# Attention: score stacks loaded in two column parts, first-pass tiles ordered by query tile, projections and statistics moved between steps

## What is computed

```python
qkv = x @ Wqkv.T + b_qkv                        # 16 heads of 32
scores = einsum('bqhd,bkhd->bhqk', q, k) * scale + alibi_bias
scores = where(causal, scores, -1e9)
p = softmax(scores, axis=-1)
ctx = einsum('bhqk,bkhd->bqhd', p, v)
return ctx @ Wout.T + b_out
```

## Time and profile before

| | us |
|---|---|
| median of 3 runs | 3004.56 (3004.28 to 3004.92) |
| the profiled execution | 3000.08 |
| its span | 2998.4 |

### The profile page before, as it was taken

How to read it: one execution, slowest core, us unless ns; L and a number is a source line. 1 busy time by engine, 2 the same in 40 slices (tenths; PEclk the granted TensorE clock), 3 DMA queues, 4 the chain that set the end, 5 groups by cost and what they waited for, 6 DMA issues and landing times. The chain is left out here.

```text
span 2998.4 us, 67154 instructions
## 1 busy us (share of the span) xinstructions
PE 2562.4 (85%) x13156; PEld 1885.8 (63%) x13157; DVE 1534.4 (51%) x3734; ACT 1375.9 (46%) x3572; POOL 1099.5 (37%) x913
## 2 busy tenths in 40 slices
PE   0229999999999378989989898998599999999994
PEld 0117888888888245555555555555378888888883
DVE  8764554555543336564564646455345555555431
ACT  0216666666655323232232323232166666666652
POOL 3434655565555200001011010101245655555552
PEclk9999999999999778998989888898799999999997
DMA  5436877888854423232332323333167787888545
GB/s 154 134 125 156 189 179 179 188 186 185 193 94 53 100 57 79 78 76 74 92 85 77 80 71 78 85 78 86 60 170 179 187 189 170 189 192 197 96 55 144
DMA packets 155637, 377.83 MB, mean 126 GB/s; under 512 B 33277, under 2 KB 34685, under 8 KB 155298
## 3 DMA queue, kind: packets, MB, share of 16 engines
q0 software_dynamic: 76416, 168.58, 29.0%
q1 hardware_dynamic: 68256, 198.28, 23.1%
q10 hardware_dynamic: 10882, 10.14, 1.1%
HBM read 236.63 MB, written 126.88 MB: 121 GB/s over the span
## 5 line engine op out<-in xcount | busy, mean ns | idle before, releaser
L504 POOL DMA_INDIRECT x_rows<-f_ob,f_it x320 | 514.3, 1607 | 573.3 <-ACT f_ob L651 240.0
L554 PE MATMUL f_psg<-f_wh,f_xh 128*128 x1280 | 535.4, 418 | 4.7 <-DVE f_xl L722 4.7
L554 PE MATMUL f_psg<-f_wh,f_xl 128*128 x1280 | 504.9, 394 | 0.0
L554 PE MATMUL f_psg<-f_wl,f_xh 128*128 x1280 | 502.1, 392 | 0.0
L496 POOL DMA_INDIRECT f_xg<-xn_rows,f_it x320 | 356.4, 1114 | 112.6 <-issue 94.5
L1309 DVE CUSTOM_DVE_ANT_0 a_psa<-a_psa,cst 128x128 f32<-128x128 f32 (+3 forms) x512 | 249.8, 504 | 189.2 <-PE a_psa L1096 186.6
L1225 ACT ACTIVATE a_pt<-a_psb 128x256 f32<-128x256 f32 (+3 forms) x512 | 213.3, 438 | 284.4 <-PE a_psb L1144 279.6
L1017 POOL CAST a_cth<-a_ct 128x512 fp32r<-128x512 f32 x32 | 19.6, 612 | 798.5 <-DVE a_ct L1333 798.5
L651 ACT ACTIVATE f_ob<-f_pso,f_wcol 128x512 f32<-128x512 f32 x320 | 220.7, 690 | 192.5 <-issue 116.1
L1096 PE MATMUL a_psa<-a_stk,a_stq 98*128 98x128 f32 (+3 forms) x512 | 230.5, 458 | 79.0 <-DVE a_mx L1309 41.9
L722 DVE TENSOR_TENSOR f_xl<-f_psx,f_xh 128x512 fp32r<-128x512 f32 x320 | 221.4, 692 | 137.3 <-ACT f_xh L632 90.7
(11 more groups left out here) (186 smaller groups left out, 4383.6 us busy)
## 6 DMA issues: line engine op xcount, KB each, us to landing
f_wraw<-w_in SPq DMA_DIRECT2D x128, 768.0 KB
a_stq<-a_qk SPq DMA_DIRECT2D x128, 192.0 KB
a_stk<-a_qk SPq DMA_DIRECT2D x128, 192.0 KB
r_xt<-x_in SPq DMA_DIRECT2D x32, 256.0 KB, 4.4
xn_rows<-r_xo SPq DMA_DIRECT2D x32, 256.0 KB, 2.9
a_xt<-x_rows SPq DMA_DIRECT2D x8, 1024.0 KB, 5.2
a_x<-x_rows SPq DMA_DIRECT2D x8, 1024.0 KB, 5.5
x_rows<-a_x POOLq DMA_DIRECT2D x8, 1024.0 KB, 5.0
```

What stands on the lines that cost most here:

```text
L504: g.indirect_dma_start(x_d, bass.IndirectOffsetOnAxis(it[:, n:n + 1], 0), ob[:, n % OB, :], None, compute_op=ALU.add).then_inc(s_sca[n % O ...
L554: mm = pe.matmul(psg[:, j, :], x[:, j, k, :], w[:, cols], start=(k == 0 and n == 0), stop=(k == DC - 1 and n == 2))
```

## The change

1. Stacks are loaded in two column parts: columns 0 to 383 of all rows once B tiles 0 to 11 of the slot's old owner are done, then columns 384 to 511 once all 16 are; ten DMAs each, so 20 per u instead of 10, of 3/4 and 1/4 the size. Each part has its own semaphore (`s_stk`, `s_stl`); `high` waits for both.
2. A tiles run by query tile (four heads of 128 columns, then of 256, 384, 512), two per step in steps 0 to 2 and one per step in 3 to 12. Tile 0 waits for part one, tile 12 (the first with 512 columns) for part two.
3. `turn_maxima` is in step 15, ahead of the last context products; the values of the next batch come after it.
4. q of u+2 is projected ahead of the steps as before, k in four chunks of three products in steps 0, 1, 3 and 5.
5. ScalarE makes high of q after exp 1 and high of k after exp 7; VectorE makes low of q after maximum 4, low of k after maximum 11. The statistics are placed one tile at a time after maxima 5, 7, 9 and 12 (the last with the moments). The turns of x are in steps 9, 10, 12 and 14; VectorE's rows after maxima 5, 6, 8, 9 and the low halves after 12 to 15. VectorE's `normalise` always comes after `negated`.

```diff
+    LATE = S - P
+    A_AT = {0: (0, 1), 1: (2, 3), 2: (4, 5), 3: (6,), 4: (7,), 5: (8,), 6: (9,), 7: (10,), 8: (11,), 9: (12,),
+            10: (13,), 11: (14,), 12: (15,)}
+    K_AT = {0: 0, 1: 1, 3: 2, 5: 3}
+    X_AT = {9: 0, 10: 1, 12: 2, 14: 3}
+    STATS_AT = {5: (0,), 7: (1,), 9: (2,), 12: (3, TB)}
+    ROW_AT, LOW_AT = {5: 0, 6: 1, 8: 2, 9: 3}, {12: 0, 13: 1, 14: 2, 15: 3}
...
                     sp.wait_ge(s_qh, u + 1)
-                    if not below(u, 2):
-                        sp.wait_ge(s_b, u * 16 - 16)
-                    for j in range(HG):
-                        rows = slice(j * HD, (j + 1) * HD)
-                        for n, to in enumerate((stq, stk)):
-                            sp.dma_start(raw(to[0:3 * HD, slot + j, :]), raw(qk3[rows, n, :, :])).then_inc(s_stk, 16)
-                    for r in range(2):
...
+                    for done, cols, told in ((12, slice(0, LATE), s_stk), (16, slice(LATE, S), s_stl)):
+                        if not below(u, 2):
+                            sp.wait_ge(s_b, u * 16 - (32 - done))
+                        for j in range(HG):
+                            rows = slice(j * HD, (j + 1) * HD)
+                            for n, to in enumerate((stq, stk)):
+                                sp.dma_start(raw(to[0:3 * HD, slot + j, cols]), raw(qk3[rows, n, :, cols])
+                                             ).then_inc(told, 16)
+                        for r in range(2):
...
+                def scores_row(u, slot, *tiles):
+
+                    for i in tiles:
+                        t, h = i // HG, slot * HG + i % HG
+                        if i == 0:
+                            pe.wait_ge(s_stk, u * STK + STK)
+                        if t == TB - 1 and i % HG == 0:
+                            pe.wait_ge(s_stl, u * STK + STK)
+                        if not (below(u, 1) and i < 2):
+                            pe.wait_ge(s_am, u * 16 + (i - 1))
...
+                    if p_on:
+                        out = take(bk, "q", g)
...
+                        project(out, (g + 2) % NG, 0, range(DC)).then_inc(s_w, 1)
                     pe.wait_ge(s_mr, u * 32 + 32)
...
+                            if a_on and n in A_AT:
+                                scores_row(u + 1, (g + 1) % 2, *A_AT[n])
                             if kt and j % 2:
                                 context(u, g, kt - 1, j // 2)
...
+                            if p_on and n in K_AT:
+                                k = K_AT[n]
+                                if k == 0:
+                                    out = take(bk, "k", g)
+                                mm = project(out, (g + 2) % NG, 1, (k,))
...
+                            if a_on and n == 15:
+                                turn_maxima(bk, u + 1, g, (g + 1) % 2)
...
                     if not below(u, 1):
                         a.wait_ge(s_stk, u * STK)
+                        a.wait_ge(s_stl, u * STK)
...
+                        for n in range(HG * TB):
+                            probability(u, n)
+                            if n in (1, 7) and not (last and g >= 2):
+                                high(bk, u + 2, g, (g + 2) % NG, n // 7)
+                            if g == 1 and n in X_AT and not last:
+                                rows_high(bk, b + 1, (X_AT[n],))
...
+                        for i in range(HG * TB):
+                            if not (last and g == 3):
+                                maximum(u + 1, (g + 1) % 2, i)
+                            if i in (4, 11) and not (last and g >= 2):
+                                low(bk, u + 2, g, (g + 2) % NG, i // 11)
+                            if g == 0 and i in STATS_AT and not last:
+                                means(b + 1, *STATS_AT[i])
```

More of the change, by code:

```diff
@@ L786, in uses @@
                 found += [("x", t) for t in range(TB)]
+            if not (last and g == 3):
+                found += [("m", g)]
             if g == 3 and not last:
                 found += [("v", t) for t in range(TB)]
-            if not (last and g == 3):
-                found += [("m", g)]
             if g == 3:
@@ L1086, in project @@
                                    [lambda k, x=x: x[:, k, :] for x in (xth, xtl)], chunks)
[L1088 to L1097, removed]
+                def scores_row(u, slot, *tiles):
[7 more added lines that the diff above has]
+                            pe.wait_ge(s_am, u * 16 + (i - 1))
+                        pe.matmul(psa[:, i % 2, 0:(t + 1) * P], stq[0:3 * HD + 2, h, t * P:(t + 1) * P],
+                                  stk[0:3 * HD + 2, h, 0:(t + 1) * P], start=True, stop=True).then_inc(s_a, 1)
                 def turn_maxima(bk, u, i, slot):
@@ L1161, in batch @@
                     for g in range(NG):
[L1162 to L1169, removed]
-                        attention(bk, b, g, a_on, g == 1 and not last)
-                        if a_on:
-                            if g == 3:
-                                values(bk, range(TB))
-                            turn_maxima(bk, u + 1, g, (g + 1) % 2)
+                        attention(bk, b, g, not (last and g >= 2), not (last and g == 3), g == 1 and not last)
+                    if not last:
+                        values(bk, range(TB))
                     output(bk, b)
@@ L1239, in batch @@
                         u = b * NG + g
[L1240 to L1247 removed]
+                        for n in range(HG * TB):
[4 more added lines that the diff above has]
+                                rows_high(bk, b + 1, (X_AT[n],))
                         if not (last and g == 3):
                             maxima(u + 1, (g + 1) % 2)
+                    if not last:
+                        values(bk)
                 bk = Bank(None)
@@ L1386, in _ @@
                 v.sem_inc(s_n2, 1)
-                means(0)
+                means(0, *range(TB + 1))
                 for t in range(TB + 2):
@@ L1395, in _ @@
                         low(bk, u, u, u, n)
-                for j in range(HG):
-                    maxima(0, 0, j)
+                for i in range(HG * TB):
+                    maximum(0, 0, i)
                 negated(bk, 0, 0)
```

109 lines of the change are left out of this document (43 added, 66 removed).

## The result

The changed kernel takes 3024.0 us (median of 9 runs, 3012.8 to 3035.1), the kernel before 3004.9 beside it; the ratio is 1.0066, with a 95% interval of 1.0054 to 1.0078. So it is 0.66% slower, where I had forecast 2990. Its profiled execution took 3016.67 us with a span of 3015.0, 16.6 above that of before.

The account below looks back on a forecast made before the run. It took the stacks' late landing, not the maxima, to set the attention's period. 7 x (1.0 - 1.5) - 6.6 - 5 = -15 us, against 3000.08 profiled gives 2985; as median 2990, range 2970 to 3012.

Parts of the forecast that it names:

- three transitions: Inside a batch, from second-pass tile 11 of one group to the next group's: 25.75 us each, together 78.0 against 77.03.
- What bounds the kernel: Attention, each u: stacks land 2.4 us late for second-pass tile 4, through high of q and exp 2, and set the period.
- The load in two parts: SP's queue: part one takes 7.3 us to issue, part two 6.1; all landed at 15.1 us, today 13.45.
- L: Time from the start of second-pass tile 11 until all stacks have landed: 15.1 us, bounds 12.9 and 18.9.
- slow queue: Rival, SP's small DMAs: 0.86 us per issue, landing at 18.9, +80 over 21 transitions, 3070 us; chance 0.22.
- cheap halves: Rival, SP's queue: twenty issues cost little more than ten, landing at 12.9 or less, 2935 us; chance 0.20.
- The maxima's chain: Between second-pass tiles 11 and 0: turn at 4.1 us, 5.7 more to tile 0 at 9.8, a new 2.4 us wait.
- The steps behind B4, and the clock: TensorE up to second-pass tile 11: ends 9.65 us after all stacks land, plus 1.0 for lower clock (bounds 0 and 1.75).
- clock: Rival: two idle stretches per u keep TensorE's clock low twice as long, +21 us in all, 3011 us; chance 0.08.
- Across the batch end: From group 3's second-pass tile 11 to that of the next batch's group 0: -1.5 us per batch.
- The -1.1 a batch: Group 0 from batch 2 on: one lower-clock stretch fewer as the statistics stall goes, -1.1 us six times.
- The edges: Ahead of the loop -1.0 us for first-pass tile 0, the rest in the last batch; together -5 us.

Follow-up runs that it names:

- late_high: Changed kernel with ScalarE's high of q after exp 5 instead of 1 and VectorE's low of q after maximum 7 instead of 4: 2907.4 us, ratio 0.9678.
- few_issues: Changed kernel with six of the twenty stack DMAs left out from u = 2 on, so some stacks keep older data: 2892.5 us, ratio 0.9626.
- high_at_3: Changed kernel with high of q after exp 3 and low of q after maximum 6: 2906.4 us, ratio 0.9679.
- Filled: Changed kernel plus eight products that nobody reads, ahead of second-pass tile 4 in groups 1 to 3: 2966.4 us, ratio 0.9868.
- split_alone: Kernel before the change with only the split of the stack load into two column parts, all orders old: 3008.2 us, ratio 1.0005.
- high_at_2: Changed kernel with high of q after exp 2 and low of q after maximum 5: 3006.3 us, ratio 1.0007.

## Why the prediction was wrong

The direction was wrong: -15 us forecast for the profiled execution, +16.6 measured, 31.7 apart. The first batch and what is ahead of it were to bring -1.5 and brought +4.4; the six periods between the stores of the loop 6 x (1.0 - 1.5) - 6.6 = -9.6, and +10.5; the last batch -4, and +0.5; behind the attention 0, and +1.2. By the rows of batches 1 and 2 I forecast 78.0 for the three transitions and 53.4 across the batch end; the means of batches 1 to 6 are 80.4 and 54.0. So most of the miss is in the transitions.

**What bounds the kernel.** Right. The load's end, through `high` and exp 2, is what B4 waits for, and late_high, few_issues and high_at_3 show that taking that away takes away the loss.

**The load in two parts.** Right, to 0.4 us. L is 14.72 (1324.57 to 1339.29), forecast 15.1. The pitch is 0.64 to 0.65 in both parts; I had 0.68 and 0.74 in part one and 0.63 in part two, and with 1.6 and 1.02 too much and too little for the pairs of small ones (1.41 and 1.30). Neither *slow queue* nor *cheap halves* came.

**The maxima's chain.** Too dear. Turn to B0 took 4.43 (1328.54 to 1332.97), not 5.7; why the rows of the last batch, from which I took it, have more I can't say. The wait of 2.4 ahead of B0 was 0.61. It moved nothing, because B4 waits for the load and not for B0: 16.38 behind B11, forecast 16.9. The stall at B4 took up what B0 had left.

**The steps behind B4, and the clock: the step that failed.** I wrote "Today a stretch at the lower clock lasts about 3.5 us and can cost at most half, 1.75; some of it falls into the waits, so I take 1.0 (bounds 0 and 1.75)". B4 to B8 took 8.09, against the 5.24 of the same steps at full clock in group 0 of batch 2: 2.85 us, outside of my bounds. Filled gives it again, 2.6. The stretch lasts 6.8 us, and lies wholly in steps with work. I had taken its length from one place in one batch; from batch 2 on the kernel before has 6.8 us at that very place, and so the bound of 1.75 was wrong by the trace that I had. The transition adds up: forecast 25.75, measured 26.94; -0.38 for L, -0.14 from there to B4, +2.66 for B4 to B8, -1.0 for the clock that I had put apart, +0.05 for B8 to B11 (2.47). The *clock* rival came nearest, with a chance of 0.08: it takes 1 us more for the low clock in each transition. But it put that to two idle stretches per u, and one was enough; and at 3011 it was still 13 too low.

**Across the batch end.** Too good. In batch 2 it is 52.64 for 54.92, -2.3 where I had -1.5; but that is the better kind of batch. Over batches 1 to 6 it is -0.5. The 3.84 us that A2 waits were foreseen; that the clock can stay low behind them for 10.2 us, in every other batch, wasn't. The -1.1 a batch had no ground either: I put the longer periods from batch 2 on to group 0, and 0.6 to 0.8 of the 1.1 lie in the transition into group 3 (25.0 for 24.29), where the low stretch is 6.8 us instead of 3.4.

**The edges.** In front of the loop I gave A0 1.0 us and looked no further. In the first u, VectorE's `low` stands ahead of the first maximum and waits, through `high`, for both parts of the stacks. TensorE's A0 and A2 there:

```profile
1078.13 0.69 PE L1106 MATMUL a_psa<-a_stk,a_stq 98*128 98x128 f32 x2 [4.33 <-DMA a_stk<-a_biases]
...
1087.70 0.72 PE L1106 MATMUL a_psa<-a_stk,a_stq 98*128 98x128 f32 x2 [8.88 <-DVE a_mx L1321]
```

A0 starts at 1078.13, 1.9 sooner than before (1080.06), but A2 is held for 8.88 us, where it was 2.49. The turn of the maxima is 3.6 later (1098.96 for 1095.35), and B0, with k's products moved behind it, 1.8 later (1119.40 for 1117.60), 1.1 of them from ahead of the attention. The first batch's three transitions then take 2.7 more. In the last batch the gains were there: its transitions into groups 2 and 3 are 3.7 and 1.3 shorter. But the ones into groups 0 and 1, with A2's and B4's waits, are 2.8 and 1.4 longer. An edge has the same in-order queues as the loop, and needs the same question, what stands behind the wait.

**What stays open.** Why nearly the same wait is followed by 3.4 us of low clock in one batch and by 6.8 in another (before the change), or by 10.2 and 3.4 in turn (A2 after it); and why split_alone gains in the transitions into groups 0 and 2. Issuing part two from another queue, so that the two parts' issues overlap, wasn't tried.

## What to carry to other kernels

When a load is split or starts sooner, ask when its last part lands and what is queued, on an in-order engine, behind whatever waits for that part; then compare with the moments at which the next engine asks for each of these instructions. These deadlines come in jumps (0.4 us and then 2.4 here), and one place further in the program was worth 3.3%, five times what the change itself moved. Price an idle stretch of TensorE by its length and by the low clock behind it, with half of the longest stretch as upper bound, looked for in every batch of the trace and not in one; a few products that nobody reads, put into the wait, tell the two apart in one run.

## What the runs showed of the hardware

- A wait of 2.75 us on TensorE was followed by 6.8 us at 0.50 of full speed, for 2.6 to 2.85 us of loss; one of 2.29 in high_at_2 by 6.8 too. In the kernel before, waits of 1.91 and 1.86 at one place, in batches 1 and 2, were followed by 3.4 and 6.8 us. Behind B0's waits of 0.37 (late_high) and 0.58 (high_at_3) the clock stayed at 1.00.
- With the same wait in the same place (A2, 3.81 to 4.16 us), the mean granted clock of the 16 us from the store on was 0.68 and 0.89 in turn, batch by batch.
- SP took 0.63 to 0.65 us to issue a DMA of 96 rows, of 144 KB or of 48 KB alike, and 1.30 to 1.41 for the two small ones together.
